# Block 0 attention of a two-block transformer kernel: two score products, one for the maxima and one with the keys on the partitions

## The chip, the cores and the metric

One core of a Trainium2 chip. The time is the device time of one launch in microseconds, here the median of three runs. PE is TensorE, DVE VectorE, ACT ScalarE, POOL GpSimd; SP issues most DMAs.

## The reference, cut to what matters

64 sequences of 128 tokens, width 256, a context of 128 tokens of width 192 for each, and a condition vector. Two transformer blocks follow each other. Block 0 has 16 heads of width 16, block 1 has 16 heads of width 64 with a rotary embedding. Each is self-attention, cross-attention, feed-forward, all with a modulated layer norm in front and a residual behind. Block 0's attention is what the change touches:

```python
def _attn(q, k, v):                    # H = 16, HD = 16
    scores = jnp.einsum('bhnd,bhmd->bhnm', q, k) * HD ** (-0.5)
    p = jax.nn.softmax(scores, axis=-1)
    o = jnp.einsum('bhnm,bhmd->bhnd', p, v)
x = x + _attn(q, k, v) @ Wos + bos                                   # pass 0
x = x + _attn(h @ Wq + bq, context @ Wk + bk, context @ Wv + bv) @ Woc + boc   # pass 1
x = x + gelu(h @ W1 + b1) @ W2 + b2                                  # pass 2
```

Everything is float32.

## The kernel before, in words

Six passes run over 16 groups of 4 sequences ("batches" below): `KIND = "aafbbf"`, self-attention, cross-attention and feed-forward of block 0 (passes 0, 1, 2), then of block 1 (3, 4, 5). Between passes x goes through a scratch tensor in HBM.

**The order is written out by hand.** `schedule()` (line 127) puts every stage of every group or batch on a tick. Each engine then walks over the ticks and, inside a tick, over the stages in the order in which its program lists them; semaphores alone hold an engine back. A tick has no length of its own: it lasts as long as its work. In passes 0 and 1 a group has 16 ticks (`STEP`), a batch 4. `T0` and `END` are the first and last ticks of the passes. Lags are counted from `tb`, the batch's tick.

**Precision.** Large products are taken as three float32r products (high x high, high x low, low x high), `three` at lines 617 to 624. So every operand is split in a high and a low half. Plain float32 products are used in few places: PV in both blocks (lines 748, 768), the scores of block 1 (line 780), and transposes by the identity.

**Block 0 attention, per group.** Q and K are projected transposed (features on partitions, 4 batches x 128 tokens along the free axis; lines 711, 724; K's bias comes from a product of its own with a row of ones, line 723). ACT and DVE split Q into `AH`, `AL` (lines 901, 1111) and K into `KBH`, `KBL` (lines 909, 910, 1118). A 32-row strip of a partition chunk holds two heads; K is kept twice, masked for the even and the odd head (`e`), so that one product of 32 rows and 256 columns gives both heads.

- Scores (line 701, lags -2 and 0): half a batch `h` is two row strips `r` = 2h, 2h+1, two chunks `c`, three products each: 12 products of 32 rows x 256 columns into banks 2h and 2h+1. Queries are on the partitions.
- Maxima (line 1065, DVE, one reduction of 128x1024 per half), then the exponential with the maximum as bias and the sum from the accumulator: 16 pieces of 128x128 per batch (line 926, ACT).
- Reciprocal of the sums (line 1078, DVE), normalization of P, 128x512 four times per batch (line 1265, POOL).
- P is transposed, 16 transposes of 128x128 per batch (line 816, PE), and copied out of PSUM (line 1073 on DVE three times, line 958 on ACT once).
- PV (line 748): 16 products with 32 columns of V as weights, 128 columns of P moving, four column strips; then the split into `OH`, `OL` (lines 917, 1125), the output projection (line 758) and the residual (line 1106).

The norm of the next group, its transposes (line 838), the context's transposes (line 849, pass 1) and their split (lines 1220 to 1222, DVE) lie on ticks between. Banks 4 to 7 are one ring (`FOUR`) for Q, K, V, P transposes, PV, outputs and transposes; banks 0 to 3 hold scores.

`WH` and `WL` hold the split weights, 8192 columns each. Block 0's W1 and W2 lie in columns 4096 to 8192, and until the scores are done the same columns hold `KBH` and `KBL`. Pass 2 (line 858 up, 872 down) uses banks 0, 1 for up and 2, 3 or 6, 7 for down.

The lines of order around the change:

```python
KIND = "aafbbf"
STEP = {"a": 16, "b": 16, "f": 8}
at["scores0", tb + 2 * h - 2].append(Half(...))
at["max0", tb + 2 * h - 1].append(Half(...))
for stage, lag in (("exp0", 0), ("normal", 1), ("p_turn", 3), ("p_copy", 4)):
```

## Time and profile before

| | |
|---|---|
| three runs | 4009.18, 4012.47, 4015.44 us, median 4012.47 |
| the profiled execution | 4010.95 us, its span 4009.1 us |
| PE, DVE, ACT, POOL busy over the span | 96%, 79%, 62%, 71% |
| chain that ended last, by engine | PE 69%, DVE 12%, ACT 8%, DMA 4%, POOL 3% |

The span runs from the first to the last instruction; the 1.9 us to the profiled execution's time lie around it. Busy times of PE include the drain of each product, which overlaps the next one's start, so what a run of products costs is read from the start of its first to the start of the next thing. In the rows below, `32*128` is rows x columns of the weights, and `x12` counts records; a plain float32 product leaves two records, a float32r product or a transpose one. Names are those of memory areas: `WH,AH` in a row of line 701 is K's high half, which lies in `WH`.

### The profile page before, as it was taken

What the parts mean: (1) busy time and instruction counts of PE and PEld (TensorE: products, weight loads), DVE (VectorE), ACT (ScalarE), POOL (GpSimd) and SP (SyncE); (2) the same over time, 40 slices, a digit from 0 to 9 for tenths busy, and PEclk for the clock granted to TensorE, in tenths of its full rate; (3) what the DMA queues carried; (4) which work ended last, traced back from release to release, by engine and by line L of the source; (5) the groups of instructions that cost most, each with busy time, mean ns of one, the idle gap of its engine ahead of it and who ended that gap; (6) DMA issues with size and microseconds to landing.
All of it is one profiled execution on the core that took longest, in us unless ns stands there. A gap on an engine that the chain in (4) does not pass through costs nothing.

```text
span 4009.1 us, 92934 instructions
## 1 busy us (share of the span) xinstructions
PE 3839.5 (96%) x32822; PEld 3295.7 (82%) x32822; DVE 3157.0 (79%) x6610; ACT 2468.4 (62%) x10244; POOL 2862.1 (71%) x2674
## 2 busy tenths in 40 slices
PE   7999999999989999999999999899999999999999
PEld 6777777777779997888888888788888888878998
DVE  7888889899985557888888888799998999975443
ACT  6999998898883334555555555455555555554333
POOL 5777877777767777666666666577777777766776
PEclk9999999999999999999999999999999999999999
DMA  2011111111111123777767677777777777772110
GB/s 81 28 33 33 33 46 41 41 49 49 54 40 54 43 64 102 219 210 219 216 212 223 208 222 225 215 213 235 223 231 222 226 231 225 231 227 85 52 43 32
DMA packets 415216, 544.98 MB, mean 136 GB/s; under 512 B 58524, under 2 KB 311968, under 8 KB 414752
## 3 DMA queue, kind: packets, MB, share of 16 engines
q1 hardware_dynamic: 267228, 404.74, 30.7%
q10 hardware_dynamic: 147524, 134.30, 12.9%
q8 instruction: 261, 4.28, 0.5%
q14 instruction: 203, 1.66, 0.1%
HBM read 220.11 MB, written 184.55 MB: 101 GB/s over the span
## 4 chain that ended last, share of the span: by engine, by line
PE 69%; DVE 12%; ACT 8%; DMA 4%; issue 3%; POOL 3%; ACTq 1%; SPq 0%; DVEq 0%
PE BANKS L621 17%; PE BANKS L622 15%; PE BANKS L623 15%; PE BANKS L780 6%; PE BANKS L768 5%; ACT PR L926 5%; PE BANKS L701 3%; PE BANKS L816 3%; DMA PB<-p_scratch 2%; DMA p_scratch<-TR 2%; PE BANKS L838 2%; DVE WL L1118 1%; DVE PT L1073 1%; POOL PR L1265 1%; DVE SN L1146 1%
## 5 line engine op out<-in xcount | busy, mean ns | idle before, releaser
L1265 POOL TENSOR_TENSOR PR<-PR,RL 128x512 f32<-128x512 f32 x1024 | 1064.1, 1042 | 602.9 <-DVE RL L1078 602.5
L942 ACT ACTIVATE PR<-BANKS,NM 128x128 f32<-128x128 f32 x2048 | 719.3, 378 | 334.5 <-DVE NM L1132 333.9
L926 ACT ACTIVATE PR<-BANKS,NM 128x128 f32<-128x128 f32 x2048 | 728.7, 414 | 12.7 <-DVE NM L1065 10.5
L621 PE MATMUL BANKS<-HH,WH 128*128 128x512 f32 x1632 | 681.4, 418 | 9.1 <-issue 7.4
L622 PE MATMUL BANKS<-HL,WH 128*128 128x512 f32 x1632 | 643.4, 394 | 0.0
L623 PE MATMUL BANKS<-HH,WL 128*128 128x512 f32 x1632 | 642.5, 394 | 0.0
L926 ACT ACTIVATION_READ_ACCUMULATOR PR<-BANKS,NM 128x1 f32 x2048 | 521.3, 255 | 0.0
L933 ACT ACTIVATE OH<-BANKS 128x512 fp32r<-128x512 f32 x256 | 153.1, 598 | 499.6 <-PE BANKS L768 257.8
L1132 DVE TENSOR_REDUCE NM<-BANKS 128x8 f32<-128x1024 f32 x256 | 310.4, 1213 | 190.4 <-PE BANKS L780 190.3
L942 ACT ACTIVATION_READ_ACCUMULATOR PR<-BANKS,NM 128x1 f32 x2048 | 445.5, 218 | 0.0
L621 PE MATMUL BANKS<-WH,OH 128*128 128x256 f32 x1280 | 375.6, 293 | 25.0 <-DVE OL L1150 20.8
L1277 POOL TENSOR_TENSOR HL<-HF,HH 128x512 fp32r<-128x512 f32 x192 | 256.3, 1335 | 171.0 <-DVE HH L1026 157.0
L621 PEld LDWEIGHTS BANKS<-HH,WH 128*128 128x128 f32 x1632 | 308.4, 189 | 84.1 <-issue 11.1
L969 ACT ACTIVATE HF<-BANKS,MODB,MODS 128x128 f32<-128x128 f32 x768 | 305.4, 487 | 115.5 <-PE BANKS L838 104.4
L816 PE MATMUL BANKS<-ID,PR 128*128 128x128 f32 x2048 | 316.9, 278 | 57.5 <-DVE OL L1125 22.0
L623 PEld LDWEIGHTS BANKS<-HH,WL 128*128 128x128 f32 x1632 | 308.3, 189 | 69.2
L622 PE MATMUL BANKS<-WL,OH 128*128 128x256 f32 x1280 | 359.9, 281 | 0.0
L1073 DVE COPY PT<-BANKS 128x512 f32<-128x512 f32 x384 | 262.9, 685 | 122.1 <-PE BANKS L816 121.0
L623 PE MATMUL BANKS<-WH,OL 128*128 128x256 f32 x1280 | 359.1, 281 | 0.0
L1085 DVE STREAM_TRANSPOSE TR<-PR 128x512 f32<-128x512 f32 x512 | 348.5, 681 | 10.3 <-POOL PR L1265 10.3
L1146 DVE TENSOR_TENSOR SN<-BANKS,ROPE 128x512 f32<-128x512 f32 x512 | 346.9, 677 | 6.1 <-DMA SW<-SN 5.9
L622 PEld LDWEIGHTS BANKS<-HL,WH 128*128 128x128 f32 x1632 | 309.3, 189 | 43.8
(134 smaller groups left out, 10692.2 us busy)
## 6 DMA issues: line engine op xcount, KB each, us to landing
SW<-SN SPq DMA_DIRECT2D x1024, 128.0 KB, 2.9
p_scratch<-TR SPq DMA_DIRECT2D x256, 512.0 KB, 4.7
PB<-p_scratch ACTq DMA_DIRECT2D x1024, 128.0 KB, 3.8
x_scratch<-X SPq DMA_DIRECT2D x80, 512.0 KB, 3.2
X<-x_scratch SPq DMA_DIRECT2D x80, 512.0 KB, 4.3
CX<-in_ctx SPq DMA_DIRECT2D x32, 384.0 KB, 4.4
X<-in_x SPq DMA_DIRECT2D x16, 512.0 KB, 4.0
out<-X SPq DMA_DIRECT2D x16, 512.0 KB, 2.9
```

The lines of the kernel that those rows point to most:

```text
L621: e.matmul(o, lh, rh, start=first and i == 0, stop=False)
L622: e.matmul(o, lh, rl, start=False, stop=False)
L623: made = e.matmul(o, ll, rh, start=False, stop=last and i == n - 1)
L816: made = e.transpose(bank[:, 128 * h:128 * h + 128], PR[npr(t)[0]][:, 128 * h:128 * h + 128], ID[:, :])
L926: made = e.activation(pr[:, r], bank[:, r], ACT.Exp, bias=nm[:, h:h + 1], accum_out=RL[npr(t)[0]][:, h:h + 1])
L942: made = e.activation(pr[:, r], bank[:, r], ACT.Exp, bias=nm[:, h:h + 1], accum_out=RL[npr(t)[0]][:, h:h + 1])
L969: made = e.activation(HF[u % 2][:, x.c, r], bank[:, r], ACT.Identity, bias=MODB[:, s, x.c, bb:bb + 1], scale=MODS[:, s, x.c, bb:bb + 1])
L1073: e.tensor_copy(PT[npt(t)[0]][:, :], PS[tp.bank(("p", t.n))][:, :]).then_inc(s_pt_d, 1)
L1085: e.transpose(TR[i % NTR][:, :].rearrange("p (j k c) -> p j k c", j=4, k=8)[:, :, 4 * e_:4 * e_ + 4, :], PR[npr(t)[0]][:, :].rearrange("p ...
L1132: e.tensor_reduce(NM[x.i % 2][:, :], BANKS[:, 2:4, :].rearrange("p e (h k) -> p (e h) k", h=4), AX, ALU.max, negate=True).then_inc(s_nm, 1)
L1146: e.tensor_tensor(SN[r % 2][:, :].rearrange("p (b t) -> p b t", b=G), src, sn, ALU.mult).then_inc(s_rt, 1)
L1265: e.tensor_tensor(p3, p3, RL[npr(t)[0]][:, :].unsqueeze(2).broadcast_to([128, 4, 128]), ALU.mult).then_inc(s_nrm, 1)
```

## The change

Block 0 alone. P is no longer transposed, and no longer normalized before PV.

- Q is kept twice with the head mask (`QB`, scaled by 0.25, bias by `BQ`), K once (`KF`, with its bias), both in plain float32, written by ACT alone. The K bias products and their operands go.
- **First product** (`scores`, lag 0 and 2, even ticks): queries on partitions, per half 8 products of 32 rows x 128 columns in float32 into banks 0 and 1. It serves the maxima only (`max0`, lags 1 and 3).
- POOL splits the negated maxima in high and low (`top`, lag 4), PE transposes them once per batch (`top_turn`, lag 5), DVE copies them with a mask (`top_out`, lag 5) into `M`.
- **Second product** (`turned_scores`, lags 7 and 9, odd ticks): keys on partitions, per half 4 products of 32 rows x 256 columns in float32 into banks 2 and 3; then 4 float32r products of 256 columns (`turned_tops`), with a selector as weights, add the negated maxima.
- The exponential (lags 8 and 10) is 128x512, four per batch, without bias and sum, straight into `PT`.
- V's unused columns hold ones instead of zeros, so PV (lag 11) gives the sums too; its 16 products now write four separate 128-column parts. `sums` (lag 12, DVE): 32x32-block transpose of 128x512 and two small reciprocals; `scale0` (lag 13, POOL): two multiplications; `back` (lag 14, DVE): transpose of 128x256; then the split, high on ACT (lag 14), low on POOL (lag 15), output product at lag 16, residual at 17.
- Pass 2 starts 4 ticks later behind pass 1. `QB` lies in the 2048 columns of W2, so W1 is split without a wait and W2 at tick END + 5, when all second products are done. Loads and norms of groups move by some ticks.

```diff
-    T0[_p + 1] = END[_p] + {1: 0, 2: 2, 4: 0}.get(_p, 0)
+    T0[_p + 1] = END[_p] + {1: 4, 2: 2, 4: 0}.get(_p, 0)
...
-            norm = tg - {"a": 26, "b": 12, "f": 8}[kind]
+            norm = tg - (26 if (p, g) == (0, 0) else {"a": 20, "b": 12, "f": 8}[kind])
...
-                    tq, tk = (tg - 17 + 4 * j, tg - 9 + 4 * j) if (p, g) != (0, 0) else (tg - 17 + j, tg - 15 + j)
-                    tq += 2 * ((p, g) == (0, 1))
+                    tq, tk = (tg - 12 + 5 * j, tg - 9 + 5 * j) if (p, g) != (0, 0) else (tg - 17 + j, tg - 15 + j)
...
-                    at["scores0", tb + 2 * h - 2].append(Half(2 * (4 * (NG * p + g) + b) + h, p, g, b, h))
-                    at["max0", tb + 2 * h - 1].append(Half(2 * (4 * (NG * p + g) + b) + h, p, g, b, h))
-                for stage, tick in (("v", tb - 3), ("v_out", tb - 2), ("pv0", tb + 8), ("high0", tb + 9), ("low0", tb + 9),
-                                    ("out0", tb + 10), ("res0", tb + 11)):
-                    for stage, lag in (("exp0", 0), ("normal", 1), ("p_turn", 3), ("p_copy", 4)):
+                    for stage, lag in (("scores0", 0), ("max0", 1), ("turned0", 7), ("exp0", 8)):
+                        at[stage, tb + 2 * h + lag].append(y)
+                for stage, lag in (("v", -3), ("v_out", -2), ("top", 4), ("top_turn", 5), ("top_out", 5), ("pv0", 11), ("sums", 12), ("scale0", 13),
+                                   ("back", 14), ("high0", 14), ("low0", 15), ("out0", 16), ("res0", 17)):
+                    at[stage, tb + lag].append(x)
...
-    chunks += [(e1 - 17, "W1", 0), (e1 - 13, "W1", 1), (e1 - 2, "W2", 0), (e1 - 1, "W2", 1)]
+    chunks += [(e1 - 17, "W1", 0), (e1 - 13, "W1", 1), (e1 + 5, "W2", 0), (e1 + 5, "W2", 1)]
...
+            def scores(x, c, e_):
+                for r in (2 * x.h, 2 * x.h + 1):
+                    rows = slice(32 * r, 32 * r + 32)
+                    made = e.matmul(PS[r % 2][:, 256 * c + 128 * e_:256 * c + 128 * e_ + 128], QB[ga % 2][rows, c, e_, s], KF[ga % 2][rows, c, s],
+                                    start=True, stop=True)
...
+            def turned_scores(y, c):
+                for r in (2 * y.h, 2 * y.h + 1):
+                    rows = slice(32 * r, 32 * r + 32)
+                    e.matmul(PS[2 + r % 2][:, 256 * c:256 * c + 256].rearrange("p (e n) -> p e n", e=2), KF[ga % 2][rows, c, s], QB[ga % 2][rows, c, :, s],
+                             start=c == 0, stop=False)
...
+            def turned_tops(y, c):
+                for r in (2 * y.h, 2 * y.h + 1):
+                    rows = slice(32 * r, 32 * r + 32)
+                    made = e.matmul(PS[2 + r % 2][:, 256 * c:256 * c + 256].rearrange("p (e n) -> p e n", e=2), SEL[rows, c, :], M[y.i // 2 % 2][rows, :, :],
+                                    start=False, stop=c == 1)
...
+                    q.wait_ge(s_nm0, x.i)
+                    q.wait_ge(s_m, y.i // 2 + 1)
+                    q.wait_ge(s_exp, 2 * y.i)
...
-                    bank = PS[tp.bank(("k", p, g, j))]
-                    e.matmul(bank[:, :], BK[:, p, 128 * j:128 * j + 128], ONES[:, :], start=True, stop=False)
-                    project_t(key, col0 + 128 * j, h, bank, False).then_inc(s_k, 1)
+                    project_t(key, col0 + 128 * j, h, PS[tp.bank(("k", p, g, j))]).then_inc(s_k, 1)
...
+                    for k in range(4):
+                        for r in range(4):
+                            h = 8 * (k // 2) + 2 * r + k % 2
+                            made = e.matmul(bank[32 * r:32 * r + 32, 128 * k:128 * k + 128], V[vi % NV][:, 32 * h:32 * h + 32],
+                                            PT[(4 * vi + r) % NPT0][:, 128 * k:128 * k + 128], start=True, stop=True)
...
-                        made = e.transpose(bank[:, 128 * h:128 * h + 128], PR[npr(t)[0]][:, 128 * h:128 * h + 128], ID[:, :])
...
+                    for r in (2 * x.h, 2 * x.h + 1):
+                        e.activation(PT[(4 * (x.i // 2) + r) % NPT0][:, :], PS[2 + r % 2][:, :], ACT.Exp).then_inc(s_exp, 1)
...
-                    for h in range(4):
-                        r = slice(128 * h, 128 * h + 128)
-                        made = e.activation(pr[:, r], bank[:, r], ACT.Exp, bias=nm[:, h:h + 1], accum_out=RL[npr(t)[0]][:, h:h + 1])
...
+                    e.transpose(TO[vi % 2][:, :, :, :, :].rearrange("p c e q d -> p (c e q d)"), PS[tp.bank(("pv", x))][:, :]).then_inc(s_to, 1)
+                        made = e.reciprocal(RC[vi % 2][:, :, e_, :], TO[vi % 2][:, :, e_, :, 16 - 16 * e_])
...
+                    e.transpose(OF[vi % 2][:, :], NO[vi % 2][:, :]).then_inc(s_of, 1)
```

## Rows read from the trace of the kernel before

**Rows 1.** The page: granted TensorE clock in forty slices, tenths of full speed
```profile
PEclk9999999999999999999999999999999999999999
```

**Rows 2.** Windows over single groups, pass 0 twice, pass 1 twice; columns above
```profile
core 0: us, PE busy (x) PEld busy (x) DVE busy (x) ACT busy (x) POOL busy (x), PEclk, DMA share, GB/s
309.18:344.05 34.87, 32.80 (x373) 27.71 (x371) 29.58 (x68) 32.28 (x152) 27.70 (x29) 1.00 0.10 32
448.59:483.44 34.85, 32.77 (x373) 27.69 (x371) 29.58 (x68) 32.27 (x152) 27.68 (x29) 1.00 0.10 32
843.64:879.73 36.09, 33.02 (x375) 27.74 (x373) 32.72 (x73) 32.40 (x152) 27.66 (x29) 1.00 0.15 46
987.98:1024.06 36.08, 33.02 (x375) 27.75 (x373) 32.73 (x73) 32.38 (x152) 27.69 (x29) 1.00 0.15 46
```

**Rows 3.** PE timeline, one pass-0 group: start us, length us, engine, what, count
```profile
309.18 1.08 PE L748 MATMUL BANKS<-PT,V 128*32 128x128 f32 x32
310.19 0.66 PE L816 MATMUL BANKS<-ID,PR 128*128 128x128 f32 x4
...
312.93 0.63 PE L816 MATMUL BANKS<-ID,PR 128*128 128x128 f32 x4 [1.00 <-DVE OL L1125]
...
313.70 0.38 PE L701 MATMUL BANKS<-WH,AH 32*128 32x256 f32 x2
313.92 0.28 PE L701 MATMUL BANKS<-WL,AH 32*128 32x256 f32 x2
314.04 0.28 PE L701 MATMUL BANKS<-WH,AL 32*128 32x256 f32 x2
...
314.60 0.39 PE L621 MATMUL BANKS<-WH,OH 128*128 128x256 f32 x1
...
315.41 0.60 PE L816 MATMUL BANKS<-ID,PR 128*128 128x128 f32 x4
315.85 0.38 PE L838 MATMUL BANKS<-ID,Z 128*128 128x128 f32 x2
315.98 0.48 PE L723 MATMUL BANKS<-ONES,BK 128*128 128x512 f32 x1
...
317.67 0.60 PE L816 MATMUL BANKS<-ID,PR 128*128 128x128 f32 x4
```

**Rows 4.** PE timeline around Q's six products in a later group
```profile
604.73 0.60 PE L816 MATMUL BANKS<-ID,PR 128*128 128x128 f32 x4
605.09 0.48 PE L621 MATMUL BANKS<-HH,WH 128*128 128x512 f32 x1
...
606.56 0.60 PE L816 MATMUL BANKS<-ID,PR 128*128 128x128 f32 x4
```

**Rows 5.** PE timeline in block 1: its PV and its scores, then a projection
```profile
2000.57 1.09 PE L768 MATMUL BANKS<-PB,V 128*64 128x128 f32 x16
2001.59 1.16 PE L780 MATMUL BANKS<-KT,QT 64*128 64x128 f32 x16
2002.68 0.50 PE L621 MATMUL BANKS<-HH,WH 128*128 128x512 f32 x1
```

**Rows 6.** Weight loads by line, 75 to 1200 us, then 1500 to 2500 us
```profile
L748 PEld LDWEIGHTS BANKS<-PT,V 128*32 128x32 f32 x4064 | 103.3, 110 | 19.8 <-issue 3.3
...
L780 PEld LDWEIGHTS BANKS<-KT,QT 64*128 64x128 f32 x1872 | 114.5, 189 | 26.4 <-issue 26.1 <-POOL QT L1272 0.2
...
L768 PEld LDWEIGHTS BANKS<-PB,V 128*64 128x64 f32 x1808 | 96.4, 137 | 16.6 <-issue 5.0 <-DMA PB<-p_scratch 1.5
```

**Rows 7.** Groups by line and form, 300 to 1500 us: busy us, mean ns
```profile
L926 ACT ACTIVATE PR<-BANKS,NM 128x128 f32<-128x128 f32 x1584 | 563.4, 413 | 4.1 <-DVE NM L1065 4.0
L1265 POOL TENSOR_TENSOR PR<-PR,RL 128x512 f32<-128x512 f32 x398 | 412.5, 1043 | 208.8 <-DVE RL L1078 208.5
...
L1065 DVE TENSOR_REDUCE NM<-BANKS 128x8 f32<-128x1024 f32 x197 | 238.6, 1211 | 1.2 <-PE BANKS L701 0.7
...
L985 ACT ACTIVATE GF<-BANKS,COL 128x512 f32<-128x512 f32 x107 | 73.6, 688 | 201.8 <-PE BANKS L623 201.8
...
L1222 DVE TENSOR_TENSOR HL<-BANKS,HH 128x512 fp32r<-128x512 f32 x32 | 22.1, 691 | 1.1
```

More of the change, by code:

```diff
@@ L251, in build @@
         STG = [sb(f"STG{i}", [128, 1024]) for i in range(NSTG)]
-        WH = sb("WH", [128, 8192], R)
-        WL = sb("WL", [128, 8192], R)
+        WH, WL, QB = [], [], []
+        for side, w in (("H", WH), ("L", WL)):
+            w.append(sb(f"W{side}0", [128, 6144], R))
+            with ExitStack() as early:
+                QB.append(sb(f"QB{side}", [128, 2, 2, 512], stack=early))
+            w.append(sb(f"W{side}1", [128, 2048], R))
         X = [sb(f"X{i}", [128, G, D]) for i in range(NX)]
@@ L455, in build @@
                 tp.add(("k1", x.i), THREE if x.i > 1 else TWO, s_rt, 2 * x.i + 2)
-            for t in at["p_turn", tick]:
-                tp.add(("p", t.n), FOUR, *pt_done(t))
             for stage in ("turn", "c_turn"):
@@ new lines, in _ @@
+                for y in turned:
+                    q.wait_ge(s_sel, 1)
+                    q.wait_ge(s_m, y.i // 2 + 1)
+                    q.wait_ge(s_exp, 2 * y.i)
+                for c in range(2):
+                    for x in halves:
+                        scores(x, c, 0)
+                    for y in turned:
+                        turned_scores(y, c)
+                    for x in halves:
+                        made = scores(x, c, 1)
+                        if c == 1:
+                            made.then_inc(s_s0, 1)
@@ new lines, in _ @@
+                for c in range(2):
+                    for y in turned:
+                        made = turned_tops(y, c)
+                        if c == 1:
+                            made.then_inc(s_ts, 1)
+                for x in at["pv0", tick]:
+                    vi = 4 * xq(x.p, x.g) + x.b
+                    q.wait_ge(s_exp, 4 * vi + 4)
+                    q.wait_ge(s_vd, vi + 1)
+                    q.wait_ge(*tp.free(("pv", x)))
+                    bank = PS[tp.bank(("pv", x))]
+                    for k in range(4):
[3 more added lines that the diff above has]
+                                            PT[(4 * vi + r) % NPT0][:, 128 * k:128 * k + 128], start=True, stop=True)
+                    made.then_inc(s_pv0, 1)
@@ L705, in _ @@
+                for x in at["top_turn", tick]:
+                    vi = 4 * xq(x.p, x.g) + x.b
+                    q.wait_ge(s_topl, vi + 1)
+                    q.wait_ge(*tp.free(("top", x)))
+                    e.transpose(PS[tp.bank(("top", x))][:, 0:128], TOP[vi % 2][:, :, :].bitcast(F).rearrange("p r n -> p (r n)"), ID[:, :]).then_inc(s_tt, 1)
                 for p, g, j in at["q", tick]:
@@ L897, in _ @@
+                for p, g, j in at["q_out", tick]:
                     ga = xq(p, g)
                     q.wait_ge(s_q, 2 * ga + j + 1)
-                    q.wait_ge(s_col, 1)
-                    q.wait_ge(s_s0, 8 * ga - 8)
-                    e.activation(AH[ga % 2][:, j, :], PS[tp.bank(("q", p, g, j))][:, :], ACT.Identity, bias=col("bq" if p else "bqk", j)).then_inc(s_ah, 1)
-                for p, g, j in at["k_high", tick]:
+                    q.wait_ge(s_bq, 2)
+                    q.wait_ge(s_ts, 8 * ga - 8)
+                    for e_ in range(2):
+                        made = e.activation(QB[ga % 2][:, j, e_, :], PS[tp.bank(("q", p, g, j))][:, :], ACT.Identity, bias=BQ[:, p, j, e_:e_ + 1],
+                                            scale=MASK[:, e_:e_ + 1])
+                    made.then_inc(s_qb, 1)
@@ L1342, in _constants @@
     rope = np.tile(np.stack([cs / 8, sn / 8, cs, sn], axis=1), (2, 1, 1)).astype(f)
[L1343 removed]
+    row = np.arange(128)[:, None] % 32
+    mask = np.concatenate([0.25 * (row // 16 == np.arange(2)), (row < 8) & (row % 2 == np.arange(2)), (row < 8) & (row % 4 // 2 == np.arange(2))],
+                          axis=1).astype(f)
     return {"c_ident": np.eye(128, dtype=f), "c_mask": mask, "c_rope": rope}
```

277 lines of the change are left out of this document (126 added, 151 removed).

## The prediction

> **What bounds the kernel now.** I read the page's slices first, then the table of windows over single groups, then the PE timeline inside a group. The granted clock reads 9 tenths or more in all forty slices, the 2.4 GHz level [rows 1], so the clock is no part of this. The change touches block 0 alone, and both its passes are periodic: from one start of PV products (line 748) to the one a group later it is 34.87 and 34.85 us in pass 0 and 36.09 and 36.08 in pass 1; the windows are cut there, and their counts of records agree [rows 2]. In such a period PE is busy 32.8 to 33.0 us and ACT 32.3 to 32.4; DVE 29.6 and 32.7, POOL 27.7 [rows 2]. Nobody has much room, and ACT's share is the exponential in 64 pieces of 128 columns, 413 ns each, overlapping, plus an accumulator read [rows 7].
>
> Busy time on PE is modelled with the drain, so I price PE's pieces from start to next start [rows 3]. The 12 score products of half a batch take 0.90 (313.70 to 314.60). Inside, the step from one pair of 32-row products to the next is 0.118, for 256 columns of float32r; the x2 says that two row groups start together. Six 256-column products take 0.81, the PV block 1.01 (309.18 to 310.19), four transposes of P 0.44 (315.41 to 315.85), K's bias product with the six behind it 1.69 [rows 3]; four transposes ahead of 512-column work 0.36, Q's six products 1.47 [rows 4]. I take 0.43 for four transposes. A change of tile shape costs about 0.20: 0.90 is 6 x 0.118 and 0.19 more.
>
> Sum for a pass-0 group: scores 8 x 0.90 = 7.2; P transposes 16 x 0.43 = 6.9; PV 4 x 1.01 = 4.0; Q 2.9; K 2 x 1.69 = 3.4; V and output products 8 x 0.81, less a little, = 6.4; transposes of Z 1.0; together **31.9**. The period is 34.86, so 3.0 us of a group is waiting, 1.00 of it the visible gap at 312.93 behind the low half of the attention output [rows 3]. Pass 1 (context products with one product less, context transposes 0.9 more) sums to 31.8 against 36.08: 4.3 of waiting.
>
> **The change, part by part.** Two things happen: the other engines are relieved, and PE gets more work.
>
> Removed on PE per group: scores 7.2, P transposes 6.9, two bias products, 0.44 net of the slower start of what follows (1.69 against 1.47). Total 14.5.
>
> Added, first product (keys along the free axis, for the maxima): per half 2 x 2 x 2 products of 128 columns in true float32. A float32 matmul has two records in the trace. Block 1 has the same shape with 64 rows: 8 products, 16 records, two row groups, from 2001.59 to 2002.68, **1.09** [rows 5]. 8 x 1.09 = 8.7.
>
> Added, second product (keys on the partitions): per half 2 x 2 products of **256** columns in float32 and 2 x 2 float32r products that add the maxima. The latter are the old pair step, 2 x 0.118 = 0.24. For float32 on 256 columns the trace has no row. Bounds of the record step: not under the 0.118 of a 256-column float32r record, and not above twice the 128-column step, 2 x 0.109 = 0.218 (PV: 1.01 less 0.13 for the start, over 8 steps [rows 3]). I take **0.218**. What decides is whether 0.109 is streaming or weight load. PV loads 32 columns of weights (110 ns each), block 1's PV 64 columns (137) and its scores 128 (189) [rows 6], and all three advance at the same 0.11: 1.01, 1.02 and 1.09 us for eight record steps each [rows 3, 5]. The load shrinks and the step does not, so the step is the stream's, and 256 columns take two. Then a half is 4 x 0.218 + 0.24 + 0.20 = **1.31**, and 8 are 10.5. With 0.118 it would be 0.91 and 7.3.
>
> The Trainium skill bears on this in "FP8 and Floating Point Precision", TensorE Precision Notes: true float32 takes four passes through the array. At one column per cycle that makes 256 columns an estimated 0.43 us a product, 0.21 a record; the 128-column step of the trace agrees, no row shows 256. It is a rule against this change: the old three float32r products cost three passes, the new two float32 products eight.
>
> Smaller PE terms: in three of eight places both kinds stand side by side (same tile shape, ticks 2-3, 6-7, 10-11), -3 x 0.20 = -0.6; transposes of the maxima 4 x 0.1 = 0.4 (a step inside four transposes is 0.11); Z transposes next to tile changes 0.45 more; three neighbours of full-array work now joined, -0.3. PV keeps 16 products of 128 columns, now four separate outputs: 0.
>
> Sum: 31.9 - 14.5 + 8.7 + 10.5 - 0.6 + 0.4 + 0.45 - 0.3 = **36.5** in pass 0, 36.4 in pass 1. So PE's bare work is already longer than the whole old periods of 34.86 and 36.08.
>
> Other engines, per group. ACT loses the 64 pieces and 4 copies and gets 16 exponentials of 128x512 at about the 688 ns of the Gelu [rows 7]; the pieces fill some 20 us of the 32.3 in [rows 2], so about 21 remain. DVE loses 12 copies and 6 low halves of 512 columns, 4 of 256 and 16 small reciprocals, 10,240 columns; it gets per batch a transpose of 512, one of 256, a masked product of 256 and two small reciprocals, 4,096. At the 1.35 ns a column of the context split (691 over 512 [rows 7]) that is some 8 us less: 21 in pass 0, 24 in pass 1. POOL loses 16 x 1.04 = 16.7 [rows 7] and gets eight scalings of 128 columns, four low halves of 256 and eight tiny ones: at its 2.04 ns a column 4.2, some 6 with their starts, so about 17. All lie beside PE's 36.5 and cost nothing while they keep their place in the order.
>
> **Waits that are left.** The maxima have one pair of banks (0, 1): product, drain, 1.21 us of reduction [rows 7], next product; some 1.5 us must be covered by what PE does in the odd tick. The tightest is the second product, 1.1 next to the first, and PV, 1.0: covered. The exponentials (banks 2, 3) need 2 x 0.69 and the drain, some 1.7, against 2.0 at least. In pass 0 I find 0.3 us a group (a Z transpose takes the bank of an output product whose residual add sits behind the masked product on DVE). In pass 1 DVE does the context split, twice 0.69 per half [rows 7], in ticks 1 and 2; behind it stand the bank of the second context transpose and the next maximum. V waits about 1.1 for the residual add, the context transpose about 1.0 for the split: 2.1 a group. Queued behind these on PE is the next first product, which then finds its maximum ready.
>
> Periods: 36.8 and 38.5. Differences: 16 x (36.8 - 34.86) = 31, 16 x (38.5 - 36.08) = 39. Edges: at the start PE already waits for other engines behind the first scores, so coming two ticks later in the order costs 0, and at most the few us that those waits last; two DMAs of a row less, 0; earlier or later loads of X stay ticks ahead of their use, 0. At the end W2 is split only after the last second product: 2 copies on ACT and one subtraction on DVE of 1024 columns (1.2 each by the 1.21 of the maximum's 1024) against two up-projections (2.8) of cover, 1 to 2 us, and four thin ticks before the FFN, 1 to 2: **+3**. The FFN and block 1 keep their work. Sum 31 + 39 + 3 = +73, on the profiled execution's 4010.95: 4084. The median of the three runs is 1.5 higher; I say **4085**.
>
> **Rivals.**
> 1. *PE's wide float32 is load-bound.* Place: the 256-column records of the second product; 4 steps in each of 256 halves. If such a record takes 0.118, PE saves 256 x 4 x 0.10 = 102 us: 4085 - 102 = **3983**, faster. It decides below a record step of 0.218 - 74/1024 = 0.146. For it: 128-column weights do take 189 ns to load, and nothing wider than 128 columns was ever streamed in float32 here. Against it: the same 0.11 with loads of 32, 64 and 128 columns [rows 3, 5, 6]. The Trainium skill's page "TensorE: Matmul & The Clock Gate", LDWEIGHTS, gives load time by columns, an estimated 27 ns for 32 and 107 for 128; the means in the trace differ by about that much, which is why the constant step speaks for the stream. Chance 0.15.
> 2. *The waiting stays what it was*, 3.0 and 4.3 us a group instead of 0.3 and 2.1: the longer chain (product, maximum, split on POOL, transpose, mask, product, exponential, PV, three transposes) hands the wait on. 16 x (2.7 + 2.2) = 78 more: **4160**. For it: today PE waits although no engine is full. Against: every link has a tick of about 2.3 us, and the loads fall to 17 to 24 of 37. Chance 0.13.
> 3. *No waiting at all*: 16 x (36.5 - 34.86 + 36.4 - 36.08) + 3 = 34: **4045**. Chance 0.15.
> 4. *The pairs do not run together in float32*, so it isn't two row groups at a time: each of the 512 half-batch products would take about 1 us more: near 4600. The 64-row pairs of block 1 run together [rows 5]. Chance 0.01.
>
> My forecast has 0.51; the remaining 0.05 is mistakes in my small terms that happen to bring it level. **Range** 4030 to 4165: it holds the forecast with both ends of its small terms, rival 3 and rival 2; rival 1 and the level cases, 0.2 together, stay outside. Within 0.2% (8 us, about what a measurement of this kernel can tell) is 0.05, faster 0.15, slower 0.80.
>
> **What would show it.** In the profile after: the period of a group's PV block (36.8, 38.5); the second product's records stepping by 0.218 against 0.118 per pair; the first product at 1.09 a half; ACT about 21, POOL about 17 busy us a group; PE without gaps in pass 0 and a 1 us gap at the context transposes in pass 1, released by DVE. Wrong if the wide records step under 0.15, if a group shows 3 us of gaps, or if the FFN starts many us later than the sum of the periods says.

## The result, and the profile after

The changed kernel takes **4164.66 us** (median of 4 runs, 4159.05 to 4168.51), the kernel before on the same chip 4013.95: a ratio of 1.0372, with a 95% interval of 1.035 to 1.0394. It is slower by 150.7 us. The forecast was 72.5 us slower than the median shown before, so the sign is right and the size is half of what came; 4164.66 lies at the very edge of the range. The profiled execution took 4168.51 us, its span is 4166.5.

The page of the changed kernel: busy time of each engine, then the granted clock in forty slices, then the chain of work that ended last, by engine.

```profile
PE 4022.2 (97%) x34934; PEld 3430.0 (82%) x34934; DVE 2935.7 (70%) x6035; ACT 1996.1 (48%) x6534; POOL 2583.5 (62%) x2803
...
PEclk9999998999998999999999999999999999999999
...
PE 81%; DVE 8%; DMA 3%; ACT 3%; issue 2%; POOL 2%; ACTq 1%; SPq 0%; DVEq 0%; POOLq 0%
```

PE is now busy nearly all the time, and two slices of the clock fell under 9 [rows 1]. The table of windows over single groups, cut from one start of PV products (now line 743) to the one a group later, as in [rows 2]: one group of pass 0, two of pass 1 that follow each other.

```profile
core 0: us, PE busy (x) PEld busy (x) DVE busy (x) ACT busy (x) POOL busy (x), PEclk, DMA share, GB/s
290.88:328.95 38.07, 36.93 (x439) 30.56 (x437) 22.78 (x51) 17.41 (x34) 18.87 (x33) 1.00 0.09 29
...
974.24:1014.35 40.11, 37.08 (x441) 30.60 (x439) 26.05 (x56) 17.41 (x34) 18.89 (x33) 1.00 0.13 41
1014.35:1059.87 45.52, 43.11 (x441) 35.38 (x439) 26.35 (x56) 17.41 (x34) 18.91 (x33) 0.85 0.12 36
```

Three things stand in these rows. PE's busy time in a group went from 32.8 to 36.9 us in pass 0 and from 33.0 to 37.1 in pass 1. Beside it is 1.1 us of idle time in pass 0 and 3.0 in pass 1; the same view of the kernel before leaves 2.1 and 3.1 [rows 2], so the idle time halved in pass 0 and stayed in pass 1, at other places. And the third window has the same 441 records as the second, in 5.4 us more, at a granted clock of 0.85: part of that group ran at 1.2 GHz.

**Where the 157.6 us between the two profiled executions are.** I cut both traces at the same work. Fourteen periods of pass 0: 14 x (38.07 - 34.86) = +45. Sixteen of pass 1 at full clock: 16 x (40.12 - 36.08) = +65. The same sixteen groups took 29.3 us more than 16 x 40.12 (671.2 from 596.88 to 1268.11), against 1.1 in the kernel before: **+28**, the low clock. The start and the last two groups: +7, where the forecast has 3 for the edges and twice 1.94 for two groups of pass 0. From the first down product of the FFN to the end: 2828.8 against 2816.1, **+13**, in stages whose lines were not edited.

The kernel before had a low clock too, in one of its sixteen groups of pass 1, in a place that its forty slices do not show:

```profile
697.69:735.39 37.70, 34.63 (x375) 29.19 (x373) 32.73 (x73) 32.50 (x152) 27.65 (x29) 0.95 0.14 44
```

The PE timeline of the group of the first window: start us, length us, engine, line, what, count.

```profile
291.89 1.16 PE L666 MATMUL BANKS<-KF,QBH 32*128 32x128 f32 x16
292.98 0.50 PE L614 MATMUL BANKS<-HH,WH 128*128 128x512 f32 x1
...
295.30 1.13 PE L675 MATMUL BANKS<-QBH,KF 32*128 32x256 f32 x8
296.08 0.59 PE L682 MATMUL BANKS<-M,SEL 32*128 32x256 f32 x4
296.60 0.33 PE L751 MATMUL BANKS<-ID,TOP 128*128 128x128 f32 x1
...
306.76 0.82 PE L666 MATMUL BANKS<-KF,QBL 32*128 32x128 f32 x10
307.32 0.48 PE L675 MATMUL BANKS<-QBH,KF 32*128 32x256 f32 x2
...
307.64 0.37 PE L675 MATMUL BANKS<-QBH,KF 32*128 32x256 f32 x1
...
307.85 0.60 PE L675 MATMUL BANKS<-QBH,KF 32*128 32x256 f32 x4
308.10 0.59 PE L682 MATMUL BANKS<-M,SEL 32*128 32x256 f32 x4
308.61 1.08 PE L743 MATMUL BANKS<-PT,V 128*32 128x128 f32 x32
...
311.18 0.50 PE L614 MATMUL BANKS<-HH,WH 128*128 128x512 f32 x1 [0.40 <-POOL HL L1313]
...
315.77 1.16 PE L666 MATMUL BANKS<-KF,QBL 32*128 32x128 f32 x16
317.53 1.10 PE L675 MATMUL BANKS<-QBL,KF 32*128 32x256 f32 x7 [0.60 <-ACT PT L923]
...
318.83 1.08 PE L743 MATMUL BANKS<-PT,V 128*32 128x128 f32 x32
```

The first product (line 666) takes 291.89 to 292.98, 1.09. The second (lines 675 and 682) takes 295.30 to 296.60, 1.30. Where the two touch and nothing waits, both take 306.76 to 308.61, **1.85** and not 1.09 + 1.31 - 0.20 = 2.20: the second begins (307.32) while the first still runs. In the third such place the second product waits 0.60 for the exponential, and the pair takes 3.06. A second stand of this group, 0.40 at 311.18, waits for the low half of the norm on POOL. The ACT timeline says why the exponential is late.

```profile
314.96 1.45 ACT L931 ACTIVATE QBH<-BANKS,BQ,MASK 128x512 f32<-128x512 f32 x2 [5.16 <-PE BANKS L682]
316.30 1.08 ACT L923 ACTIVATE PT<-BANKS 128x512 f32<-128x512 f32 x2
```

The copies of Q (line 931) overwrite the buffer of the group two before, so they wait for that group's last second product, which ended just then. They stand ahead of the exponentials in ACT's queue, and the exponentials hold the banks of the next second product.

In pass 1 the PE timeline shows the two waits that I had forecast (0.85 and 0.84), two that I had not, and what can follow them. First the stands of the group of the second window:

```profile
989.81 0.39 PE L614 MATMUL BANKS<-WH,HH 128*128 128x256 f32 x1 [0.85 <-DVE X L1136]
...
991.73 0.66 PE L871 MATMUL BANKS<-ID,CX 128*128 128x128 f32 x4 [0.84 <-DVE HL L1232]
...
996.96 0.50 PE L614 MATMUL BANKS<-HH,WH 128*128 128x512 f32 x1 [0.62 <-POOL HL L1313]
...
1003.29 1.10 PE L675 MATMUL BANKS<-QBH,KF 32*128 32x256 f32 x7 [0.72 <-ACT PT L923]
```

This is the group of the third window.

```profile
1029.92 0.38 PE L614 MATMUL BANKS<-WH,HH 128*128 128x256 f32 x1 [0.85 <-DVE X L1136]
...
1031.84 1.12 PE L871 MATMUL BANKS<-ID,CX 128*128 128x128 f32 x4 [0.84 <-DVE HL L1232]
...
1036.34 1.94 PE L743 MATMUL BANKS<-PT,V 128*32 128x128 f32 x32
```

The PV block behind them takes 1.94 us instead of 1.08, and with it everything from 1031.84 on for several us. The same two stands occur in the group before, and there the clock stays up.

### The profile page after: what moved, and what is told of

It is laid out like the page before. It is cut to its first block, busy times and chain, and to the rows that moved or that the text cites. A ratio compares the mean times of both kernels' runs of the same rounds, so it can differ in the third digit from the quotient of the medians.

```text
span 4166.5 us, 92935 instructions
## 1 busy us (share of the span) xinstructions
PE 4022.2 (97%) x34934; PEld 3430.0 (82%) x34934; DVE 2935.7 (70%) x6035; ACT 1996.1 (48%) x6534; POOL 2583.5 (62%) x2803
## 4 chain that ended last, share of the span: by engine, by line
PE 81%; DVE 8%; DMA 3%; ACT 3%; issue 2%; POOL 2%; ACTq 1%; SPq 0%; DVEq 0%; POOLq 0%
PE BANKS L614 18%; PE BANKS L615 16%; PE BANKS L616 16%; PE BANKS L675 6%; PE BANKS L810 6%; PE BANKS L798 5%; PE BANKS L666 5%; PE BANKS L743 3%; PE BANKS L860 2%; DMA p_scratch<-TR 1%; PE BANKS L682 1%; POOL HL L1313 1%; DMA PB<-p_scratch 1%; DVE SN L1156 1%; DVE TR L1115 1%
## 5 line engine op out<-in xcount | busy, mean ns | idle before, releaser
L962 ACT ACTIVATE PR<-BANKS,NM 128x128 f32<-128x128 f32 x2048 | 720.8, 378 | 346.0 <-DVE NM L1142 345.5
L1301 POOL TENSOR_TENSOR PR<-PR,RL 128x512 f32<-128x512 f32 x512 | 533.4, 1042 | 336.7 <-DVE RL L1108 336.7
L614 PE MATMUL BANKS<-HH,WH 128*128 128x512 f32 x1632 | 690.1, 423 | 20.5 <-POOL HL L1313 11.1
L1142 DVE TENSOR_REDUCE NM<-BANKS 128x8 f32<-128x1024 f32 x256 | 310.3, 1212 | 195.0 <-PE BANKS L810 195.0
L962 ACT ACTIVATION_READ_ACCUMULATOR PR<-BANKS,NM 128x1 f32 x2048 | 444.5, 217 | 0.0
L923 ACT ACTIVATE PT<-BANKS 128x512 f32<-128x512 f32 x512 | 278.0, 596 | 275.7 <-PE BANKS L682 275.7
L982 ACT ACTIVATE HF<-BANKS,MODB,MODS 128x128 f32<-128x128 f32 x768 | 295.1, 457 | 185.3 <-PE BANKS L860 174.4
L1079 DVE TENSOR_REDUCE NM<-BANKS 128x8 f32<-128x1024 f32 x256 | 312.4, 1220 | 98.3 <-PE BANKS L666 96.0
L1115 DVE STREAM_TRANSPOSE TR<-PR 128x512 f32<-128x512 f32 x512 | 348.8, 681 | 10.9 <-POOL PR L1301 10.9
L1308 POOL TENSOR_TENSOR KT<-KT,SW 128x512 f32<-128x512 f32 x256 | 330.8, 1292 | 15.8 <-DMA SW<-SN 15.6
L1308 POOL TENSOR_TENSOR QT<-QT,SW 128x512 f32<-128x512 f32 x256 | 332.9, 1300 | 5.6 <-DMA SW<-SN 5.6
```

Of the source, the lines that this page charges most:

```text
L614: e.matmul(o, lh, rh, start=first and i == 0, stop=False)
L962: made = e.activation(pr[:, r], bank[:, r], ACT.Exp, bias=nm[:, h:h + 1], accum_out=RL[npr(t)][:, h:h + 1])
L982: made = e.activation(HF[u % 2][:, x.c, r], bank[:, r], ACT.Identity, bias=MODB[:, s, x.c, bb:bb + 1], scale=MODS[:, s, x.c, bb:bb + 1])
L1079: e.tensor_reduce(NM0[x.i // 2 % 2][:, x.h, :, :], BANKS[:, 0:2, :].rearrange("p r (h k) -> p r h k", h=4), AX, ALU.max, negate=True).then ...
L1115: e.transpose(TR[i % NTR][:, :].rearrange("p (j k c) -> p j k c", j=4, k=8)[:, :, 4 * e_:4 * e_ + 4, :], PR[npr(t)][:, :].rearrange("p (b ...
L1142: e.tensor_reduce(NM[x.i % 2][:, :], BANKS[:, 2:4, :].rearrange("p e (h k) -> p (e h) k", h=4), AX, ALU.max, negate=True).then_inc(s_nm, 1)
```

## The experiments

Each edit is against the changed kernel unless said otherwise. Twelve kernels ran.

### Q's copy a tick later

```diff
-                    at["q_out", tq + 1].append((p, g, j))
+                    at["q_out", tq + 1 + (j == 0 and (p, g) != (0, 0))].append((p, g, j))
```

> Edit: ACT copies the first Q block (j = 0) out one tick later, behind the exponentials of tick 6 instead of ahead of them. In the changed kernel PE stands 0.60 us before the second product of tick 7 (317.53), released by an exponential, and ACT had just spent 1.45 us on Q's copy, which itself waited until 314.96 for the last second product of the group two before (that product frees QB). Theory A (the Q copy delays the exponentials, and these delay PE): the gap goes, and the tick-7 product starts inside the first product of tick 6, as it does in ticks 3 and 11 (0.54 less for the two together). 0.6 + 0.5 = 1.1 us in each of 32 groups, 35 us: period 37.0 in pass 0, 39.0 in pass 1, total about 4130. Rival B (something else is due right behind, the maximum or a ring bank): the gap only moves, total within 10 us of 4165.

Measured: 4148.17 us (4131.85 to 4164.6), ratio 1.0343 [1.0305, 1.038]. Windows over one group of pass 0 and two neighbours of pass 1:

```profile
245.96:282.77 36.81, 36.28 (x438) 30.02 (x436) 22.65 (x51) 17.41 (x34) 18.85 (x33) 1.00 0.10 31
822.69:861.49 38.80, 36.49 (x441) 30.10 (x439) 25.92 (x56) 17.40 (x34) 18.88 (x33) 1.00 0.14 42
861.49:905.80 44.31, 42.62 (x441) 34.93 (x439) 26.20 (x56) 17.39 (x34) 18.90 (x33) 0.85 0.12 37
```

The period falls by 1.24 us in pass 0 and by 1.3 in pass 1: the wait for ACT (0.60) and the overlap that it destroyed. The periods are now 36.8 and 38.8, where the forecast had 36.8 and 38.5. The 0.40 behind POOL is left in pass 0. But the time falls by 16 us, and not by the 35 expected or by the 40 that the periods give, since the clock is low in 11 of the first 15 groups of pass 1, against 7 of 15 in the changed kernel.

### Context transposes at other ticks, and both edits together

```diff
-                    at["c_turn", tg - 16 + c if p == 1 else tg - 7].append(Part(p, g, c, 0))
+                    at["c_turn", tg - 14 + 2 * c if p == 1 else tg - 7].append(Part(p, g, c, 0))
-                    at["c_split", tg - 15 + c if p == 1 else tg - 6].append(Part(p, g, c, 0))
+                    at["c_split", tg - 13 + 2 * c if p == 1 else tg - 6].append(Part(p, g, c, 0))
```

> Edit: pass 1's two context transposes move from ticks 0 and 1 to ticks 2 and 4 of a group, their splits on DVE from 1 and 2 to 3 and 5. In the changed kernel every pass-1 group has gaps of 0.85 us (V product, released by the residual add on DVE) and 0.84 us (second context transpose, released by the context split on DVE) in a row, and the granted clock is at 1.2 GHz for about 100 us of pass 1, in stretches of 10 us that begin around there. Theory A (the clock falls because of these two gaps): both gaps and the low-clock stretches go: 16 x 1.7 = 27 us and some 27 us more, total about 4110, pass-1 groups all near 38.4. Rival B (the clock falls for the kind of work, 32-row products beside transposes): gaps go, stretches stay, total about 4138. Rival C (the splits only push the wait to another stage, as DVE is in order): total above 4150.

Measured: 4157.39 us (4141.59 to 4175.84), ratio 1.0367 [1.0331, 1.0404]. The two stands of 0.85 and 0.84 are gone and another of 1.34 us is there (V's products, released by the copy of Q), since the banks go round in a ring of four and V's now was Q's. Most full-clock groups take 38.7, but 10 of the first 15 run at a lower clock and take 40.3 to 43.3. Theory C fits best: the wait went to another stage.

> Both edits together. If both theories hold they add: 35 + 54 = 89 us, total about 4075, which is also what the forecast's own sum of PE work with next to no waits gives (4045 to 4085). If the waits hand each other on, less than the sum of the two.

With Q's copy later as well: 4158.68 us (4158.39 to 4166.4), ratio 1.0373 [1.0357, 1.039]. A group of pass 1 in the table of windows, and two rows of its PE timeline:

```profile
876.02:918.77 42.75, 40.23 (x441) 32.57 (x439) 26.27 (x56) 17.53 (x34) 18.86 (x33) 0.92 0.13 38
```

```profile
903.25 0.39 PE L614 MATMUL BANKS<-WH,HH 128*128 128x256 f32 x1 [2.26 <-ACT QBL L931]
...
907.00 1.93 PE L743 MATMUL BANKS<-PT,V 128*32 128x128 f32 x32
```

The bank is now held a tick longer, so the stand is 2.26 us, and in every group of pass 1 the clock is at 1.2 GHz behind it. Two waits were removed, and the program was no faster: they came back as one, in one piece.

### No wait left in pass 1

Q's copy later, as above, and the context transposes at two neighbouring ticks, both two later than in the changed kernel:

```diff
+                    at["c_turn", tg - 14 + c if p == 1 else tg - 7].append(Part(p, g, c, 0))
+                    at["c_split", tg - 13 + c if p == 1 else tg - 6].append(Part(p, g, c, 0))
```

> Edit to the changed kernel: Q's first copy on ACT one tick later, as before, and the context transposes in ticks 2 and 3 (splits 3 and 4) instead of 2 and 4. With 2 and 4 the ring of four banks gave the V product of tick 5 the bank of Q's first block, and in every pass-1 group PE stood 2.26 us there and the granted clock fell to 1.2 GHz behind it; with 2 and 3 it gets the first-but-one context bank and no PE product of a group waits long. Theory A (the clock falls because PE stands for 1 to 2 us in one place): no low-clock stretches in steady pass 1, period 36.6 to 37.2 there as in pass 0, total 4060 to 4075. Rival B (separate 32-row products are what lets the clock fall in pass 1): stretches stay, pass-1 period 39 to 42, total 4110 to 4140.

Measured: **4076.06 us** (4069.99 to 4079.53), ratio 1.0154 [1.0139, 1.017]. One group of either pass:

```profile
245.80:282.65 36.85, 36.31 (x439) 30.05 (x437) 22.66 (x51) 17.40 (x34) 18.79 (x33) 1.00 0.10 30
801.35:838.59 37.24, 36.98 (x441) 30.38 (x439) 25.91 (x56) 17.38 (x34) 18.82 (x33) 1.00 0.15 44
```

Nothing of the arithmetic changed, and 89 us went. Over 0.26 us there is no stand left in that group of pass 1, and every period of pass 1 has the full clock. In pass 0 one stand is left:

```profile
266.10 0.50 PE L614 MATMUL BANKS<-HH,WH 128*128 128x512 f32 x1 [0.40 <-POOL HL L1313]
```

So of the 150.7 us, 89 are waits and the low clock behind them. What remains is mostly PE's longer work, and the 13 us of the stages that were not edited.

### Both kinds in one tick, on four row groups

The second product of a half uses the other two 32-row groups than the first product of the half six ticks on. With an even lag both kinds are issued in one tick, turn by turn.

```diff
-                    for stage, lag in (("scores0", 0), ("max0", 1), ("turned0", 7), ("exp0", 8)):
+                    for stage, lag in (("scores0", 0), ("max0", 1), ("turned0", 6), ("exp0", 7)):
```

> Edit: one lag. The second product goes from lags 7 and 9 to 6 and 8, the exponential from 8 and 10 to 7 and 9. So in each even tick the first product of one half and the second product of the other half, on the other two row strips and in other banks, stand interleaved, four row strips at a time. Theory A (strips run independently of each other): the two need about 1.4 us together, the longer of the two plus the start, instead of 1.09 + 1.30 = 2.39, or 1.85 where they already touch. 5 separate pairs x 1.0 + 3 x 0.45 = 6.4 us less PE work a group, bare work about 30; with 1 to 3 us of waits the period is 31 to 33 and the total about 3960 to 4020, below the kernel before. Rival B (PE takes two strips at a time, or the weight loads of four strips queue up): only the shape changes are saved, 0.2 to 0.5 each, total 4080 to 4140. Rival C: the shorter ticks leave the maxima uncovered (1.09 + 1.5 us between two first products) and PE waits for DVE: gaps before the first product, total 4020 to 4080.

Measured: **3894.9 us** (3891.99 to 3898.19), ratio 0.971 [0.9692, 0.9728], faster than the kernel before. One score tick in the PE timeline, and a group of either pass:

```profile
306.59 0.38 PE L666 MATMUL BANKS<-KF,QBH 32*128 32x128 f32 x2
306.60 0.48 PE L675 MATMUL BANKS<-QBH,KF 32*128 32x256 f32 x2
...
307.90 0.44 PE L860 MATMUL BANKS<-ID,Z 128*128 128x128 f32 x2
```

```profile
211.05:240.99 29.94, 28.88 (x439) 24.27 (x437) 22.58 (x51) 17.29 (x34) 18.82 (x33) 1.00 0.12 37
676.12:708.56 32.44, 29.19 (x441) 24.28 (x439) 25.84 (x56) 17.37 (x34) 18.85 (x32) 1.00 0.17 51
```

Both products together take 306.59 to 307.90, **1.31 us**: what the second takes alone. Beside the second the first product costs nothing. Eight times (1.09 + 1.30 - 1.31) less the overlap at two seams (2 x 0.54) is 7.6 of the 8.1 us by which the period of pass 0 falls, and the wait of 0.60 at the third seam is the rest. That is more than theory A had expected (3960 at best). In pass 1 the two stands are still there (0.85 and 0.84 at 688.54 and 690.46), yet the granted clock is 1.00 here, and in all but one of the sixteen groups; that one has the same two stands:

```profile
513.16:546.38 33.22, 30.65 (x441) 25.57 (x439) 25.99 (x56) 17.37 (x34) 18.76 (x32) 0.95 0.16 49
```

The same without those two stands (context transposes at ticks 2 and 3):

> Edit: the four-strip order (second product at lags 6 and 8, exponential at 7 and 9) with context transposes in ticks 2 and 3. The four-strip kernel has 29.9 us a group in pass 0 and 32.4 in pass 1, with pass-1 gaps of 0.85 (residual add), 0.83 (context split), 0.57 (low half of the norm on POOL), 0.8 (DVE high half) and 0.32 (maximum). Theory A: the first two go, 1.7 us in 16 groups, 27 us: 3868. Rival C: with ticks of 3.7 us for two, DVE (25.6 of 32.4 busy in pass 1) is late for the maxima once the splits stand behind them in ticks 3 and 4: gain under 10 us, 3885 to 3905.

Measured: 3869.2 us (3864.99 to 3873.33), ratio 0.9641 [0.9626, 0.9655]; a group of pass 1 takes 30.83.

**Is it the alternation, or the shared tick?** In the 3869 us version I issued the two kinds one behind the other within their tick:

```diff
                     for x in halves:
                         scores(x, c, 0)
-                    for y in turned:
-                        turned_scores(y, c)
                     for x in halves:
                         made = scores(x, c, 1)
...
+                for c in range(2):
+                    for y in turned:
+                        turned_scores(y, c)
```

> The version of 3869 us (four row groups, context transposes at ticks 2 and 3) with the two kinds still in one tick, but issued one kind behind the other instead of turn by turn. Theory A, the four row groups save time only where records of both kinds alternate: the pair then takes the 1.85 us that touching kinds showed in the changed kernel instead of 1.31, so 8 x 0.54 = 4.3 us a group, periods 34.2 and 35.1, and 32 x 4.3 = 138 us: about 4007. Theory B, what counts is the shared tick (fewer changes of tile shape, fewer waits): periods stay at 29.9 and 30.8 and the time at 3869, at most 30 us more.

Measured: 3980.44 us (3976.37 to 3981.07), ratio 0.992 [0.9903, 0.9937]. The PE timeline of a pair:

```profile
321.72 0.82 PE L666 MATMUL BANKS<-KF,QBH 32*128 32x128 f32 x10
322.28 0.48 PE L675 MATMUL BANKS<-QBH,KF 32*128 32x256 f32 x2
...
323.58 1.08 PE L744 MATMUL BANKS<-PT,V 128*32 128x128 f32 x32
```

The pair takes 1.86 us, as theory A had it; the period of pass 0 is 33.8. The time rose by 111 us against the 138 expected, since a part of the longer products fills what had been waiting: 3.9 us a group in pass 0 and 3.1 in pass 1 (33.9 against 30.83), not 4.3. Between the version without waits in pass 1 (4076) and the 3869 us version lie 207 us: 111 of them hang on the turn-by-turn order, and the other 96 come with the shared tick itself (five more seams a group at 0.54 would make 86). A version with both kinds in one tick on the *same* two row groups was not tried.

**Does a stand bring the clock down here too?**

> The kernel with four row groups (3894.9 us) with Q's copy a tick later and the context transposes at ticks 2 and 4, the two edits that together left a stand of 2.26 us behind the copy of Q in pass 1 and the half clock behind it in every group of the changed kernel. Theory A, a stand of some 2 us in a group is enough to bring the clock down: the low clock comes back here, pass 1 goes from 30.8 without waits to 30.8 + 2.3 + about 4.5 = 37.6 us a group and the time to about 3869 + 16 x 6.8 = 3978. Theory B, the clock stays up in this mix and only the stand is paid: 33.1 us a group, 3869 + 16 x 2.3 = 3906. Theory C, there is no stand, since the second product no longer sits in a tick of its own ahead of Q's copy: 3870 to 3885.

Measured: 3879.4 us (3875.76 to 3882.05), ratio 0.967 [0.9656, 0.9685]. The stand behind Q's copy did not come back (0.26 us at 720.05). Instead PE stands 1.33 us for the high half of Z's transpose, which DVE rounds, and the clock stays up (periods of 31.47 throughout pass 1):

```profile
700.04:731.51 31.47, 29.20 (x440) 24.29 (x438) 25.88 (x56) 17.25 (x34) 18.83 (x32) 1.00 0.18 52
```

Theory C, then, and not the test of the clock that I wanted.

### The second layer's weights one tick earlier

In the 3869 us version:

```diff
-    chunks += [(e1 - 17, "W1", 0), (e1 - 13, "W1", 1), (e1 + 5, "W2", 0), (e1 + 5, "W2", 1)]
+    chunks += [(e1 - 17, "W1", 0), (e1 - 13, "W1", 1), (e1 + 4, "W2", 0), (e1 + 4, "W2", 1)]
```

> As x7_four_ct, and W2 is split at tick END + 4, where the last second product now is, instead of END + 5. In the four-strip kernel PE stands 6.0 us at the first down-projection while ACT loads its Gelu and exponential tables in turn (1.28 each) and DVE takes 3.57 for the two subtractions of W2. Theory: the copies start ahead of the second Gelu, 2 to 4 us earlier; total 2 to 4 us under x7_four_ct. Rival: the copy waits for the same last product and the exponentials stand in front of it on ACT: no difference.

Measured: 3861.7 us (3860.32 to 3867.46), ratio 0.9625 [0.9609, 0.9641], 7.5 less, where 2 to 4 were expected. In the changed kernel the FFN's first down product waited for W2's low half, by the PE timeline and by DVE's:

```profile
1337.74 0.36 PE L614 MATMUL BANKS<-WH,GH 128*128 128x256 f32 x1 [3.70 <-DVE WL L1260]
```

```profile
1333.92 3.72 DVE L1260 TENSOR_TENSOR WL<-STG,WH 128x1024 fp32r<-128x1024 f32 x2 [0.52 <-ACT WH L1005]
```

Both chunks are subtracted behind each other, 3.72 us, where I had counted one at 1.2. In the 3869 us version this stand is 6.56 us; here 2.21 are left.

### The buffers' places

```diff
         TB = sb("TB", [128, 4, D])
+        sb("PAD", [128, 82])
```

> The 3861.7 us version with 82 unused floats a partition ahead of the shared buffers, so that these (the FFN's GH and GL, the attention's OH and OL among them) start at a multiple of 1024 bytes in their partition instead of 696 bytes behind one; nothing else changes. Behind block 0 the changed kernel took 12.7 us longer than the kernel before, 10.9 of it in the two FFNs, where the down products of 256 columns step by 120 ns instead of 117 although no line of the FFN was edited; only the places of GH and GL moved, by 192 bytes. Theory A, the place in the partition sets it: the two FFNs fall from 385.2 and 377.5 us to at most 379.0 and 373.1, and the time by at least 11 us, to 3850 or less. Theory B, the place does not matter: the FFNs stay at 385 and 377 and the time at 3862.

> The same with 16 unused floats, so that the shared buffers stand 64 bytes further on, at the same offset within 128 and within 256 bytes as in the kernel before. Theory A, the offset within 128 or 256 bytes sets the step of the down products: FFNs at 379.0 and 373.1 us as in the kernel before, about 3851 us. Theory A', only the offset within more than 256 bytes or something else in the layout counts: another value. Theory B, the place does not matter: 385 and 377, and 3862 us.

With 82 floats: 3847.53 us (3845.01 to 3854.04), ratio 0.959 [0.9577, 0.9603]. With 16: **3845.12 us** (3843.27 to 3846.29), ratio 0.9582 [0.9569, 0.9596], the fastest of all. And 16 floats in the changed kernel itself:

> The changed kernel itself (4164.66 us) with the 16 unused floats and nothing else. Theory A, some 13 to 17 us of the 150.7 that the change cost come from the places of its buffers alone: 4148 to 4152, with the two FFNs at about 380 and 371 us and block 1 some 5 us shorter. Theory B, the gain of the padding belongs to the fast version only, or block 0's waits and its clock swallow it: 4160 or more.

4146.63 us (4140.79 to 4150.22), ratio 1.0334 [1.032, 1.0348]: 18.0 less. The table of windows over 200 us of the second FFN, in the kernel before, the changed kernel and the changed kernel with 16 floats:

```profile
3700.00:3900.00 200.00, 200.00 (x1309) 181.88 (x1308) 91.91 (x230) 72.37 (x141) 146.86 (x130) 1.00 0.15 48
```

```profile
3850.00:4050.00 200.00, 200.00 (x1294) 182.45 (x1293) 90.12 (x228) 70.64 (x137) 144.15 (x127) 1.00 0.13 43
```

```profile
3850.00:4050.00 200.00, 200.00 (x1316) 182.73 (x1315) 93.75 (x234) 70.55 (x134) 147.60 (x130) 1.00 0.13 43
```

PE has no idle time in any of them, and at the same clock does 1309, 1294 and 1316 records. From first to last down product the two FFNs take 379.0 and 373.1 us before, 385.5 and 377.5 after, and 380.1 and 371.2 with the padding: 10.9 us lost and 11.6 had back. The profiled executions are 21.9 apart; 10.4 of that lies ahead of the first down product, where the half clock lasts 24 us less in the padded run, and I don't claim it for the places. Chance or another chip is not the cause of the FFN's part: the second FFN takes 377.5 us in the changed kernel and in all nine variants of it without padding, which ran on at least three chips, and 371.2 in both kernels with 16 floats, on two others. The kernel's small buffers had grown by 48 floats, 192 bytes (NM0 8, RC 32, MASK 4, BQ 8, RL 4 less), and moved everything behind them.

## Why the forecast had the sign and half the size

**The products were priced right.** First product 1.09 against 1.09 measured; second 1.31 against 1.30. The 256-column float32 records step by 0.21 (307.64 to 307.85 above), so the 0.218 taken at the upper bound is right, and rival 1 falls. Busy time of ACT 17.4, POOL 18.9, DVE 22.8 and 26.1 a group, against some 21, 17, 21 and 24: all far under PE's, as argued. The exponential of 128x512 takes 596 ns and not the Gelu's 688:

```profile
L923 ACT ACTIVATE PT<-BANKS 128x512 f32<-128x512 f32 x512 | 278.0, 596 | 275.7 <-PE BANKS L682 275.7
```

**The sum of PE's work was right in pass 0, by two errors that cancel.** Three touching pairs were to save 0.20 each; they save 0.54, 1.0 us a group more. The projections, now cut by more changes of tile shape, take 12.8 us by the timeline where the terms add up to 12.0. That the two nearly cancel is luck. The version with no wait left in pass 1 has periods of 36.85 and 37.24. Less the stands that it still has, 0.40 and 0.26, that is 36.4 in pass 0, against 36.5 of bare work in the forecast, and 37.0 in pass 1, against 36.4. Rival 3's 4045, with 16 x 0.35 and 16 x 0.84 for the longer periods and 12.7 for the places, is 4077, and this version measured 4076: the parts add up, though the periods are its own.

**The step that failed is the one on the waits: "In pass 0 I find 0.3 us a group", and 2.1 in pass 1.** The wait behind the 0.3, for an output product's bank, is not there; PE waits 0.60 for the exponentials and 0.40 for POOL instead. In pass 1 the two waits of 2.1 came as 0.85 and 0.84, and 0.72 for the exponentials and 0.62 for POOL stood beside them. I had written that the exponentials "need 2 x 0.69 and the drain, some 1.7, against 2.0 at least", which counts the exponentials alone. Ahead of them ACT has the two copies of Q, 1.45 us, held by the release of Q's own buffer. That wait costs 0.60 and breaks up an overlap worth another 0.61, together the 1.24 that the first experiment took away. The period was missed by 38.07 - 36.8 = 1.27 in pass 0, in 14 periods 18 us, and by 40.12 - 38.5 = 1.62 in pass 1, in 16 periods 26 us. The 0.3 above Q's copy in pass 1 was not taken apart by a run, and the 0.62 behind POOL is only a candidate. The forecast's own rule, that what is queued ahead on the engine counts, was applied to DVE and not to ACT.

**The clock, said to be "no part of this", cost 28 us.** I had read it from forty slices of the kernel before [rows 1], which hide its one group at 0.95, and no rival let it change. It was a cost of the waits: PE's idle time of pass 1 came in pieces of 0.85 and 0.84 near each other, and behind them the clock fell in about half of the groups. **The places of the buffers cost 13** (a term that was not in the sum at all). The last groups and the FFN's weights came to about what was forecast, +7, but with a 3.70 us stand among them.

In sum 73 + 18 + 26 + 28 + 13 = 158, the 157.6 between the profiled executions.

**The rivals.** Rival 2, the waiting stays what it was, gave 4160, nearest to the result, and is half right. Its periods would be 39.5 and 40.7; measured are 38.07, about midway between it and the forecast, and 40.12, near it. Its 3.0 and 4.3 are periods less a sum of starts and can't be set beside the idle time of a window; in that view 2.1 and 3.1 became 1.1 and 3.0. That its 4160 comes so near is luck all the same: 41 us of the result are the clock and the places, which it does not have. Rival 4 falls: pairs run together in float32, and more than pairs.

**What stays open** is what decides whether the clock falls. Stands of 0.85 and 0.84 us are followed by the low clock in about half of the changed kernel's groups of pass 1 (in one of them it falls only behind the 0.62 and 0.73), in more of them with Q's copy later, and in one of sixteen in the version with four row groups. In the kernel before, pass 1 has stands of about 1.1 and 0.7 in nearly every group, and the clock fell in one of sixteen. With a stand of 2.26 us it falls in or behind it always; with no stand over 0.26 in pass 1 it stayed up. In pass 0 stands of 0.40 and 0.60 are followed by it in one of fourteen groups of the changed kernel, and the 0.40 alone in none of the three versions that have only this one. So stands come before it wherever it falls in these groups, and they are not enough. Shown is only that taking the stands out gave the clock back.

## What to carry to other kernels

Where a product uses part of TensorE's rows, look for other work on the other rows and issue the two turn by turn: here that one edit turned a change that was 3.7% slower into one that is 2.9% faster, where a tick of its own had left each product two of the four row groups. When an engine's work shrinks, price its queue in order all the same, with every instruction that stands ahead of the one that others wait for. And after a change that moves buffers, compare a stage that was not edited: 64 bytes of padding were worth 17 us of 3862.

## What the runs showed of the hardware that was not expected

- **Four 32-row groups work at the same time**, even with products of different kinds. 16 records of 128 columns together with 8 of 256 and 4 float32r ones take 1.31 us turn by turn; alone they take 1.09 and 1.30, and one kind behind the other in a tick 1.86. The Trainium skill states in "TensorE: Matmul & The Clock Gate", Part 3 (Packing small matmuls), that products on different row groups run at the same time. The trace agrees, for float32 products of two widths; that the order of issue decides how much of it is had, as 1.31 against 1.86 shows, is this case's own.
- **The granted clock can fall behind small stands.** The same 441 records take 40.11 us at 1.00 and 45.52 at 0.85. With no edit to the arithmetic, removing the stands gave 89 us, of which the shorter full-clock periods explain 14 x 1.2 and 16 x 2.9, 63 us; the rest is about the 28 of the low clock. What else it hangs on stays open, as said above.
- **The place of a buffer in its partition changes the step of a 256-column product.** With GH and GL 696 bytes past a multiple of 1024 the down products step by 120 ns (median from start to start in the second FFN), at 504 by 117. Moving them by 64 bytes, to 760, gave the speed back (median 118, mean 117). The offsets are counted from the sizes of the buffers allocated ahead of them; the weights, which lie further ahead, did not move. In the 3861.7 us version the FFNs took 385.6 and 377.5 us at 696, 380.2 and 371.2 at 760, and 381.6 and 372.9 at 0. Which offsets are the slow ones was not tried further, and the reason is not shown.
